# Routed row tiles fetched from a table by indirect transfers instead of one-hot gathers, in seven batches of eight

## What is computed

```
topk_idx, weights            # 2 of 8 experts for each token, so 8192 rows
flat_idx = topk_idx.reshape(-1)
routed_in = xf[flat_idx] * weights.reshape(-1, 1)
h = silu(_grouped_mm(routed_in, w1, counts)) * _grouped_mm(routed_in, w3, counts)
routed_out = _grouped_mm(h, w2, counts)
shared = silu(xf @ sw1.T) * (xf @ sw3.T) @ sw2.T
out = shared.at[flat_idx].add(routed_out)
```

## Time and profile before

| | |
|---|---|
| median of 3 runs | 243.1 us (241.94 to 243.17) |
| the profiled execution's own time | 242.11 us |
| its span, from first to last instruction | 240.4 us |
| mean granted PE clock | 0.999 of full speed |
| busy: PE, DVE, ACT, POOL | 96%, 74%, 60%, 24% |

### The profile page before, as it was taken

The page is one execution under the profiler, slowest core; times in us unless marked ns, Lnnn a source line. Parts: engine busy times, 40 slices in busy tenths (PEclk is TensorE's granted clock), DMA queues, the critical chain, the costliest instruction groups (busy, mean ns, idle before and its releaser), DMA issues.

```text
span 240.4 us, 4667 instructions
## 1 busy us (share of the span) xinstructions
PE 230.6 (96%) x1553; PEld 204.5 (85%) x1553; DVE 177.1 (74%) x580; ACT 145.3 (60%) x390; POOL 57.5 (24%) x108
## 2 busy tenths in 40 slices
PE   6799999999999999999999999999999999999991
PEld 4789898998988989889899998898988879899760
DVE  3489658887987898878767976668586777769635
ACT  2445655755648557465575643877869686788711
POOL 3320721815508236072011000002020120202022
PEclk9999999999999999999999999999999999999999
DMA  6599420020200200000000000110845638375465
GB/s 183 189 323 307 138 87 3 5 84 4 87 4 0 87 3 1 1 3 0 0 3 0 1 3 3 48 40 11 203 73 155 115 108 169 78 189 86 140 121 180
DMA packets 18726, 19.45 MB, mean 81 GB/s; under 512 B 1032, under 2 KB 17680, under 8 KB 18704
## 3 DMA queue, kind: packets, MB, share of 16 engines
q1 hardware_dynamic: 15008, 15.50, 20.3%
q0 software_dynamic: 3696, 3.67, 10.0%
HBM read 14.95 MB, written 4.21 MB: 80 GB/s over the span
## 4 chain that ended last, share of the span: by engine, by line
PE 90%; DVE 4%; issue 1%; DMA 1%; ACT 1%; POOL 1%; DVEq 0%; ACTq 0%
PE bank L390 82%; PE bank L479 4%; PE bank L440 3%; DMA x_ring<-in_L_attn_x 1%; PE bank L412 1%; DVE x_ring L1349 1%; PE bank L431 1%; DVE bn L945 1%; DVE w L1343 1%; PE bank L547 1%; DVE xT_lo_all L936 1%; POOL rstd L307 0%; DVE arena L936 0%; DVE w L1265 0%; ACT w L885 0%
## 5 line engine op out<-in xcount | busy, mean ns | idle before, releaser
L390 PE MATMUL bank<-xT_hi_all,arena 128*128 128x512 f32 (+3 forms) x256 | 80.3, 369 | 0.0
L390 PE MATMUL bank<-arena 128*128 128x256 f32 (+2 forms) x560 | 75.9, 282 | 0.4 <-ACT attn_all L723 0.3
L390 PEld LDWEIGHTS bank<-arena 128*128 128x128 f32 (+1 forms) x560 | 71.0, 183 | 5.3 <-DVE arena L936 1.1
L723 ACT ACTIVATE arena<-bank 128x512 fp32r<-128x512 f32 (+4 forms) x84 | 36.3, 452 | 28.9 <-PE bank L390 27.4
L390 PEld LDWEIGHTS bank<-xT_hi_all,arena 128*128 128x128 f32 x256 | 47.0, 189 | 6.1 <-DVE arena L936 0.2
L936 DVE TENSOR_TENSOR arena<-bank,arena 128x264 fp32r<-128x264 f32 (+4 forms) x83 | 41.3, 507 | 14.3 <-ACT arena L723 14.1
L390 PE MATMUL bank<-xT_lo_all,arena 128*128 128x512 f32 (+3 forms) x128 | 45.8, 358 | 0.0
L376 POOL DMA_DIRECT2D x_ring<-in_L_attn_x x7 | 9.2, 1311 | 88.8 <-DVE x_ring L1284 88.8
L390 PEld LDWEIGHTS bank<-xT_lo_all,arena 128*128 128x128 f32 x128 | 24.2, 189 | 2.1
L723 ACT ACTIVATE attn_all<-bank,row_inv 128x256 f32<-128x256 f32 x32 | 15.2, 475 | 15.6 <-PE bank L390 14.7
L747 ACT ACTIVATE probs<-bank,neg_max 128x128 f32<-128x128 f32 (+3 forms) x32 | 17.0, 531 | 9.4 <-DVE neg_max L985 9.4
(11 more groups left out here) (125 smaller groups left out, 376.4 us busy)
## 6 DMA issues: line engine op xcount, KB each, us to landing
x_ring<-in_L_attn_x SPq DMA_DIRECT2D x8, 512.0 KB, 3.4
x_ring<-in_L_attn_x POOLq DMA_DIRECT2D x7, 512.0 KB, 5.8
out<-x_ring SPq DMA_DIRECT2D x7, 512.0 KB, 3.4
spread<-pairs SPq DMA_DIRECT2D x14, 128.0 KB, 3.4
w_sb<-in_L_ffn_w SPq DMA_DIRECT2D x1, 1024.0 KB, 10.9
raw_sw<-in_L_ffn_sw SPq DMA_DIRECT2D x3, 256.0 KB, 4.3
x_ring<-in_L_attn_x SPq DMA_DIRECT2D x2, 256.0 KB, 3.0
raw_qkv<-in_L_attn_WQ SPq DMA_DIRECT2D x1, 256.0 KB, 4.1
```

What stands on the lines that cost most here:

```text
L390: return nc.tensor.matmul(dst, lhsT, rhs, start=start, stop=stop, skip_group_check=True, **kw)
L723: return nc.scalar.activation(dst, src, ACT.Copy, scale=scale)
```

## The change

For batches 1 to 7 the gather is done by transfers. The table A is also kept in fp32: ACT copies it unsplit (`A_full`), PE turns it in one more transpose beside L646, ACT copies it out (`A_rows`, 64 rows of 128 values) and SP stores it as a DRAM table of 64 rows of 512 B. DVE makes integer row numbers for all row tiles (`pair_ids`, one instruction). POOL then issues an indirect transfer for each row tile: 128 rows of 512 B, each row number read from its partition, into `fetched`, which lies over the tile `xn` of stage 1. There are 8 for a batch, 56 in all, issued one batch ahead, in POOL's list before add_x of the batch before. There is one buffer for each group: a fetch for batch i waits until silu_rows of batch i - 1 has read the group. `silu_rows` waits for the four transfers (`rows_in0`, `rows_in1`) and reads `fetched`.

Gone are for i = 1 to 7 the one_hot instructions of DVE, the gather matmuls of PE and their waits, the turning of the pair numbers, their copy and store, and the 14 broadcast loads. Batch 0 stays as it was.

```diff
-            sp.wait_ge(s["pairs_kept"], 1)
-            sp.dma_start(pairs_dram, pair_T[:, :]).then_inc(s["pairs_out"], 16)
-            sp.wait_ge(s["pairs_out"], 16)
-            load_pairs(1)
-            load_pairs(2)
+            sp.wait_ge(s["a_rows_kept"], 1)
+            sp.dma_start(A_dram, A_rows[:, :]).then_inc(s["a_stored"], 16)
             for i in range(B - 2):
-                if i + 3 < B:
-                    load_pairs(i + 3)
                 store(i)
...
+            def fetch_rows(i, g):
+                if i > 1:
+                    pool.wait_ge(s["rows_silu"], RB * (i - 1) + RG * (g + 1))
+                for j in range(RG):
+                    r = i * RB + g * RG + j
+                    pool.indirect_dma_start(fetched[:, g, j, :], None, A_dram,
+                                            bass.IndirectOffsetOnAxis(pair_ids[:, r:r + 1], 0)).then_inc(s[f"rows_in{g}"], 16)
+
+            pool.wait_ge(s["x_turned"], C * B)
+            pool.wait_ge(s["a_stored"], 16)
+            pool.wait_ge(s["ids_ready"], 1)
+            fetch_rows(1, 0)
+            fetch_rows(1, 1)
             for i in range(B - 1):
+                if i + 2 < B:
+                    fetch_rows(i + 2, 0)
+                    fetch_rows(i + 2, 1)
                 add_x(i)
...
-            nc.tensor.transpose(x_bank[0][:, 0:P], A_T[:, :].bitcast(F32), ident[:, :]).then_inc(s["a_turned"], 1)
+            nc.tensor.transpose(x_bank[0][:, 0:P], A_T[:, :].bitcast(F32), ident[:, :])
+            nc.tensor.transpose(x_bank[0][0:PAIRS, P:2 * P], A_full[:, :], ident[:, :]).then_inc(s["a_turned"], 1)
...
@@ step2 of PE
                 accumulate(i - 1, 0)
-                gather(i, 0)
                 hidden(i, 1, 0, h1_bank, "h1_done")
                 shared_out(i - 1, 1)
-                gather(i, 1)
...
@@ ACT
+            copy(A_full[:, :], x_bank[0][:, 0:PAIRS])
             copy(A_T[:, 0:PAIRS], x_bank[0][:, 0:PAIRS]).then_inc(s["a_split"], 1)
             keep_attn(b, 3)
             act.wait_ge(s["a_turned"], 1)
+            copy(A_rows[:, :], x_bank[0][0:PAIRS, P:2 * P]).then_inc(s["a_rows_kept"], 1)
...
             def silu_rows(i, g):
                 act.wait_ge(s["route"], ROUTED)
-                act.wait_ge(s["gathered"], 2 * i + g + 1)
+                if i > 0:
+                    act.wait_ge(s[f"rows_in{g}"], 16 * RG * i)
+                else:
+                    act.wait_ge(s["gathered"], g + 1)
...
@@ DVE
             h_mult(0, 0)
+            nc.vector.tensor_scalar(pair_ids[:, :], pair_rows[:, :], 8.0, None, ALU.add).then_inc(s["ids_ready"], 1)
             one_hot(0, 0)
...
             def step2(i):
-                one_hot(i, 0)
                 rows_low(i - 1, 1)
                 gate_attn(i - 1, 0).then_inc(s["gated"], 1)
-                one_hot(i, 1)
```

More of the change, by code:

```diff
@@ L148, in build @@
         pair_rows = sb("pair_rows", [P, NR], BF16)
-        pair_T = sb("pair_T", [NR, P], BF16)
-        spread = sb("spread", [P, 2, RG * P], BF16)
-        pairs_dram = nc.dram_tensor("pairs", [NR, P], BF16).ap()
+        pair_ids = sb("pair_ids", [P, NR], mybir.dt.uint32)
+        A_full = sb("A_full", [P, PAIRS])
+        A_rows = sb("A_rows", [PAIRS, P])
+        fetched = xn[:, :, :].rearrange("p t d -> p (t d)").rearrange("p (g r h) -> p g r h", g=2, r=RG)
+        A_dram = nc.dram_tensor("A_table", [PAIRS, H], F32).ap()
         gs = sb("gs", [P, NT, G])
@@ L194, in build @@
             bc_done one_hot_done gathered rows_silu rows_hi rows_lo pair_one_hot_done accumulated0 accumulated1
-            inv_part wqk_loaded sum_ready sum_turned pairs_ready last_tile_done last_gate_done last_gated last_added pairs_turned pairs_kept pairs_out spread0 spread1 last_summed bias_loaded""".split()
+            inv_part wqk_loaded sum_ready sum_turned pairs_ready last_tile_done last_gate_done last_gated last_added a_rows_kept a_stored ids_ready rows_in0 rows_in1 last_summed bias_loaded""".split()
         s = {n: sem(n) for n in names}
@@ L613, in shared_out, with spread_pairs @@
                 ins.then_inc(s["o_done"], 1)
-            def turn_pairs():
-                mm(acc_bank[0:NR, 3 * P:4 * P], pair_rows[:, :], ident_bf[:, :], True, True).then_inc(s["pairs_turned"], 1)
-            def spread_pairs(g):
+            def spread_pairs(i, g):
                 if g == 1:
-                    pe.wait_ge(s["one_hot_done"], g)
+                    pe.wait_ge(s["one_hot_done"], 1)
                 for j in range(RG):
                     r = g * RG + j
-                    ins = mm(bc_bank[:, j * P:(j + 1) * P], pair_rows[:, r:r + 1].to_broadcast([P, P]), ident_bf[:, :], True, True)
+                    ins = mm(bc_bank[:, j * P:(j + 1) * P], pair_rows[:, bass.ds(i * RB + r, 1)].to_broadcast([P, P]), ident_bf[:, :], True, True)
                 ins.then_inc(s["bc_done"], 1)
@@ L628, in gather @@
                 pe.wait_ge(s["one_hot_done"], 2 * i + g + 1)
-                if g == 1 or i > 0:
-                    pe.wait_ge(s["rows_silu"], RB * i + RG * g)
+                if g == 1:
+                    pe.wait_ge(s["rows_silu"], RG)
                 for j in range(RG):
@@ L662, in _ @@
             pe.wait_ge(s["rows_ready"], 1)
-            turn_pairs()
-            spread_pairs(0)
+            spread_pairs(0, 0)
             hidden(0, 1, 0, h1_bank, "h1_done")
@@ L667, in _ @@
             gather(0, 0)
-            spread_pairs(1)
-            pe.wait_ge(s["pairs_kept"], 1)
+            spread_pairs(0, 1)
             table(1, 3)
@@ L865, in silu_rows @@
                     r = g * RG + j
-                    nc.scalar.activation(row_silu[:, g, j, :], g_bank[:, j * H:(j + 1) * H], ACT.Silu,
+                    rows = fetched[:, g, j, :] if i > 0 else g_bank[:, j * H:(j + 1) * H]
+                    nc.scalar.activation(row_silu[:, g, j, :], rows, ACT.Silu,
                                          scale=w_rows[:, bass.ds(i * RB + r, 1)]).then_inc(s["rows_silu"], 1)
@@ L888, in _ @@
             silu_hidden(0, 0)
-            act.wait_ge(s["pairs_turned"], 1)
-            copy(pair_T[:, :], acc_bank[0:NR, 3 * P:4 * P]).then_inc(s["pairs_kept"], 1)
             h_high(0, 0)
@@ L1250, in one_hot @@
             def one_hot(i, g):
[L1251 to L1257, removed]
+                dve.wait_ge(s["bc_done"], g + 1)
+                nc.vector.tensor_scalar(one_hot_T[:, g, :], bc_bank[:, :], pair_of_partition[:, 0:1], None,
                                         ALU.is_equal).then_inc(s["one_hot_done"], 1)
```

## The result

The changed kernel takes 258.15 us, median of 4 runs (254.06 to 262.60), against 242.52 us for the kernel before beside it: ratio 1.056, 95% interval 1.049 to 1.064. All ratios here leave out runs that lie over 1.5% above the fastest of the same kernel; here they are 259.77 us, the profiled one, and 262.60, so that this ratio rests on 254.06 and 256.53. So it is 13 to 15 us slower. The forecast had the direction and the engine, with 246.6 us; the size was four times as large.

The account below looks back on a forecast made before the run. PE bound the kernel before; with 1.2 us fetches POOL becomes the bound. The span grows by about 3.5 us, 242.11 to 245.6 profiled; the median, 243.1 + 3.5, is 246.6 us. Range of 8 in 10: 236.5 to 262.

Parts of the forecast that it names:

- POOL's list becomes the bound: On POOL, 8 fetches and one add_x take 10.9 us a period, more than PE's 10.28 before; chance 0.44.
- PE's part: On PE, 56 gather matmuls of 0.115 us go: 6.4 us less, 0.92 us of each period.
- ACT, DVE and SP set no new bound: DVE loses 6.9 us off the bound, ACT's copies are covered, SP is relieved; DVE and ACT together 0, 0.5 us either way.
- a cheap fetch: Rival on POOL: fetches below 1.1 us, POOL keeps up and PE's saving shows, 236.7 to 241.5 us; chance 0.32.
- a break-even: Rival on POOL: fetches of 1.10 to 1.15 us give back just what PE saved, 241.9 to 244.3 us; chance 0.10.
- Between these ends I take 1.2: POOL's price for one indirect fetch, taken as 1.2 us between ends of 0.32 and 1.5.
- POOL's sum: POOL never idle from 160.05 us: 48 fetches of 1.2 and 5 add_x of 1.28 make 64.0 us; span grows 3.5.
- wait for silu_rows(1, 0), and last landing: On POOL, fetch(2, 0) waits until silu_rows(1, 0) ends at 160.05; the last fetch lands about 2 us after issue.
- c: The unknown price of one indirect transfer on POOL; change in time = 3.5 + 48 (c - 1.2) us.
- The reason I gave for leaning up: On POOL, an instruction that software has to unpack likely has most of its cost fixed, so the price leans to 1.5 us.
- rival 3: Fetches reading row numbers from SBUF meet DVE's instructions and cost 1.6 us: +22.7, 266 us; chance 0.14.
- The queue behind the new waits: add_x behind POOL's fetches comes 4.5 us late; silu_out waits for its store two batches later, with about 4.8 us to spare.

Follow-up runs that it names:

- e1: The changed kernel with all 56 fetches and the wait on them left out (routed values wrong): 235.69 us, ratio 0.979 to the kernel before.
- e5: The changed kernel with each indirect fetch replaced by a plain POOL transfer of the same shape, reading x: 235.15 us, ratio 0.975 to the kernel before.
- e8: The changed kernel with five of a batch's eight row tiles fetched and three gathered on PE: 238.96 us, ratio 0.990 to the kernel before.
- e10: The changed kernel with six of a batch's eight row tiles fetched and two gathered on PE: 242.40 us, ratio 1.004 to the kernel before.
- e13: The changed kernel itself, run again on another occasion with six runs: 257.04 us, ratio 1.061 to the kernel before; its profiled execution took 255.50 us.
- e6: The changed kernel with each of the 56 fetches taking only 64 of its 128 rows: 251.74 us, ratio 1.044 to the kernel before.
- e3: The changed kernel with all fetches issued, but silu_rows neither waiting for them nor reading them: 254.98 us, ratio 1.058 to the kernel before.
- e2: The changed kernel with add_x moved ahead of the second group's four fetches: 261.97 us, ratio 1.079 to the kernel before.
- e9: The changed kernel with short matmuls of zeros filling PE's idle time, 12 a batch and 36 around accumulate(7, 0): 258.52 us.
- e12: The changed kernel with only the 36 short filling matmuls of zeros around accumulate(7, 0) on PE: 256.41 us, interval 1.053 to 1.065.

## Why the prediction was off

**What held.** That POOL's list becomes the bound, PE idle behind it, POOL busy from the first fetch to the last with no wait; that PE's part is worth about 6 us where nothing else binds (e1: 5 to 6). That ACT, DVE and SP set no new bound fits the traces, though silu_rows, for which I counted no change, takes 0.391 us in place of 0.368. The rivals of a cheap fetch and of a break-even are excluded by the price; both are seen as soon as fetches are plain (e5) or fewer (e8, e10).

**What failed** is the step "Between these ends I take 1.2", and with it two smaller terms of POOL's sum. The sum had the span grow by 3.5 us. It grew by 13.3 us in e13's execution (255.50 us) and by 17.5 in the first one (259.77 us). By the sum's own steps, with the difference from the prediction in brackets:

| step | predicted | e13 | first execution |
|---|---|---|---|
| POOL's first fetch starts | 149.3 | 148.96 (-0.3) | 151.41 (+2.1) |
| 55 fetches, start to start | 1.2 each | 1.318 each (+6.5) | (81.2 - 8.85) / 55 = 1.316 each (+6.4) |
| 5 add_x between them, to the next fetch | 1.28 each | 1.77 each (+2.4) | 1.77 each (+2.4) |
| wait for silu_rows(1, 0), and last landing | 1.15 and 3.2 | none, and 3.3 (-1.0) | none, and 3.3 (-1.0) |
| silu_rows(7, 1) to the reduction | 4.95 | 239.02 - 233.57 = 5.45 (+0.5) | 241.62 - 235.92 = 5.70 (+0.7) |
| reduction to DVE's last instruction | 10.26 | 10.25 (0.0) | 253.52 - 241.62 = 11.90 (+1.6) |
| from there to the end of the span | 2.7 | 4.4 (+1.7) | 4.4 (+1.7) |
| together | | +9.8 | +14.0 |

(81.2 us is from the first fetch's start, 151.41, to the last one's, 232.63; 8.85 is 5 x 1.77, an add_x of 1.45 to 1.48 us and the 0.30 before the next fetch.) The first fetch's start moves with stage 1: the transpose of `A_T` starts at 142.44 us before, at 141.27 in e13 and at 143.72 in the first execution; in both, the fetch comes 7.7 us after it, where the prediction had 6.9.

Nine tenths of the miss in e13's execution, and two thirds in the first, are POOL's prices, 8.8 to 8.9 us. What the first has on top is a later stage 1 and the lower clock of PE in the tail. I had bounded c by 1.5 and forecast the change as 48 (c - 1.2), so a hundred nanoseconds were worth 5 us, and I took a value from the middle without making the likeliest time carry what the bound said. The measured pitch, 1.316, lies between 1.2 and that end; put into the sum with add_x at 1.77 it gives 3.5 + 5.6 + 2.4 = 11.5 us, or 253.6 us for a profiled execution; e13's took 255.50, and most of the 1.9 us between them is the later end of the span, 1.7. So the path was right, and the size was wrong.

The reason I gave for leaning up, that most of an instruction's cost is fixed, was half right. It is fixed in the rows (e6), but it isn't the cost of any transfer of POOL: a plain one of 128 rows takes 0.54 us (e5), and, if the two may be compared, 0.74 of add_x's 1.28 us go with its 384 rows more (an estimate: its rows are also twice as long, and it accumulates). From those rows alone c would have come out too low; what I had for the row numbers, 0.24 us from a small elementwise instruction, should have been 0.7 (0.94 + 0.30 - 0.54). Nor is 0.24 us the smallest such instruction of POOL: its `var_eps` takes 0.20 us, which would have moved the bound by 0.04. The figure of about 620 ns that the Trainium skill gives for a transfer issued by GpSimd ("SBUF — State Buffer", "A bandwidth-pool intuition that's wrong (but worth ruling out)") is nearer to e5's 0.54 us than to the 0.94 of the indirect ones, which is the kind this kernel needs.

Three things were missing altogether. POOL's idle 0.30 us ahead of every indirect fetch is in no row of before, since nothing indirect is in it. The end of the span comes 1.7 us later behind DVE's last instruction. And PE's clock: I priced PE's stand-still at nothing beyond itself, and it was worth 0.5 to 2.4 us.

**Waiting on DVE (rival 3)** doesn't have the price that I gave it: the median fetch took 0.968 us, the fastest 0.940. But its mechanism can't be called absent. Together the 56 fetches took 5.4 to 5.6 us more than 56 x 0.94, or 0.1 us each, and the long ones stand beside DVE instructions with two inputs. In e13's execution 12 fetches behind the first took 1.18 us or more; through all of the first 0.94 us of 9 of these such a DVE instruction was running, and of the 43 shorter ones this holds for 6. From POOL's and DVE's timelines of e13:

```profile
175.94 1.23 POOL L373 DMA_INDIRECT xn<-A_table,pair_ids  x1 [0.30 <-issue]
177.47 0.94 POOL L373 DMA_INDIRECT xn<-A_table,pair_ids  x1 [0.30 <-issue]
...
175.67 0.68 DVE L938 TENSOR_TENSOR arena<-w,arena 128x512 fp32r<-128x512 f32 x1
176.33 1.14 DVE L1271 SCALAR_TENSOR_TENSOR arena<-w,w_rows,arena 128x128 fp32r<-128x128 f32 x4
```

Where a fetch stands in its batch doesn't explain it: in e3 and e10 DVE's instructions fall at other places, and the long fetches are mostly found there. Still, some of the six took only 0.94 to 0.95 us, and no run takes DVE's instructions away. So it is a likely cause and not a shown one, and it bounds rival 3 at about 0.1 us a fetch here.

**The queue behind the new waits.** I said that the late add_x "just fits" at 1.2. At 1.32 it does not: ACT waits for stores in 4 places, 11.3 us. Whether that costs anything beside the late rows is open: without these waits nothing came back (e2), and with them alone the kernel was as slow (e3).

## What to carry to other kernels

An engine at a quarter of its time is free for as long as what it is given takes less than one period of the loop it joins: multiply the new instructions by their price for one round of the loop and compare that with the period, before asking what the other engine saves. Here 8 x 1.32 + 1.77 against 10.3 loses 6%, 5 x 1.32 + 1.77 against 9.7 gains 1%, and one fetch more than that, which fills the period, takes the gain away; so give such an engine a share that leaves part of the period idle. How small that part may be is not shown; here 1.3 us of 9.7 were enough. Where the one unknown price is multiplied by 50, measure it first with one instruction, or forecast near the dear end.

## What the runs showed of the hardware

- An indirect transfer issued by POOL, 128 rows of 512 B: 0.94 us of POOL at the least and 0.97 in the median, and 0.30 us idle before it, also behind a plain transfer; 0.89 us at the least for 64 rows. It landed 3.5 us after issue (3.0 to 5.2). A plain one of the same shape: 0.54 us, no idle time before it, landed after 2.2 us.
- Fetches beside DVE instructions with two inputs took up to 1.34 us in e13's list (and the second of the list 1.48); that the one causes the other is likely and not shown.
- add_x, an accumulating transfer of 512 rows, takes 1.28 us in the median alone, 1.36 behind plain fetches (e5) and 1.45 behind indirect ones.
- silu_rows, 128 x 128 values on ACT, took 0.391 us an instruction reading SBUF and 0.367 reading a bank of PSUM, both in the changed kernel.
- The end of the span comes 2.7 us after DVE's last instruction in the kernel before, in e1 and with 28 or 35 fetches; 3.3 us with 42 and 4.4 us with 56, indirect or plain (e5, e6, e12, e13). The last stores land 1.9 to 2.3 us after issue in all of them. The trace shows nothing in the rest, and no run explains it.
- PE's granted clock was 0.65 over 9 us of the first execution in which PE was busy for 4.9, behind 3.43 us of standing still, 0.79 over 8 us of e13's in which it was busy for 4.7, and 1.00 in the same place with most of the idle time filled by matmuls nobody reads (e9, e12).
